# A graph kernel of eight rounds: another place for VectorE's list load, and one-hots that compare with a kept table

## The reference

```python
def _sage_conv(x, src, dst, Wl, bl, Wr, n_nodes):
    msg = x[src]
    summed = segment_sum(msg, dst, num_segments=n_nodes)
    cnt = segment_sum(ones((src.shape[0],)), dst, num_segments=n_nodes)
    mean = summed / maximum(cnt, 1.0)[:, None]
    return mean @ Wl + bl + x @ Wr
...
x = _layernorm(x + _L0_gnn_ref(...))   # three SAGE layers
x = _layernorm(x + _L1_gnn_ref(...))   # GIN: gelu(x[src] + edge_emb) * edge_weight, summed at dst, two-layer MLP
x = _layernorm(x + _L2_gnn_ref(...))   # two GCN layers, normalised by degree, layer norm with gain and shift
x = _layernorm(x + _L3_gnn_ref(...))   # two relational layers: one weight matrix for each of 8 edge types
```

## Time and profile before

| | |
|---|---|
| three runs | 5371.6, 5383.45 and 5387.2 us, median 5383.45 |
| the profiled execution | 5378.48 us, of which the span is 5376.4 |
| granted TensorE clock in it, mean | 0.944 of full speed |
| rounds 0 to 7, from their first one-hots | 471, 395, 579, 896, 610, 776, 750 and 852 us |

### The profile page before, as it was taken

The page is one execution under the profiler, slowest core; times in us unless marked ns, Lnnn a source line. Parts: engine busy times, 40 slices in busy tenths (PEclk is TensorE's granted clock), DMA queues, the critical chain, the costliest instruction groups (busy, mean ns, idle before and its releaser), DMA issues.

```text
span 5376.4 us, 129953 instructions
## 1 busy us (share of the span) xinstructions
PE 4387.9 (82%) x25128; PEld 2875.8 (53%) x25129; DVE 3446.8 (64%) x10510; ACT 2416.5 (45%) x4969; POOL 1921.9 (36%) x1886
## 2 busy tenths in 40 slices
PE   6998997777878888867777688887799996888895
PEld 4664554433445555535554355543577773677672
DVE  5553454787545555449997688876566663777774
ACT  2442442555257777526664466664222211333332
POOL 5650782654033333016550443310433312333310
PEclk9999999899889999989999899998899999999997
DMA  4663884665234444325553466653444433443432
GB/s 142 217 210 117 260 270 149 195 192 174 90 122 147 149 146 145 111 96 171 174 172 103 145 210 205 211 173 109 137 136 137 140 116 109 129 130 125 128 100 76
DMA packets 443919, 815.61 MB, mean 152 GB/s; under 512 B 70872, under 2 KB 76818, under 8 KB 443828
## 3 DMA queue, kind: packets, MB, share of 16 engines
q1 hardware_dynamic: 389172, 697.28, 38.4%
q0 software_dynamic: 54656, 117.32, 8.9%
HBM read 480.10 MB, written 334.22 MB: 151 GB/s over the span
## 4 chain that ended last, share of the span: by engine, by line
PE 46%; issue 15%; DVE 14%; DVEq 8%; ACT 7%; POOL 5%; DMA 3%; ACTq 2%; SPq 1%; POOLq 0%
PE p_agg L1132 8%; PE p_edge L1119 7%; PE p_agg L1134 7%; PE p_tr L1119 6%; POOL raw L696 4%; PE p_agg L1165 4%; DVE onehot L1566 4%; DVE stats L1658 3%; ACT u L916 2%; PE p_wide L1252 2%; ACT o L897 2%; DVEq L373 2%; PE p_agg L1158 2%; DVEq L1566 2%; PE p_dense L1208 2%
## 5 line engine op out<-in xcount | busy, mean ns | idle before, releaser
L1566 DVE TENSOR_SCALAR onehot<-iota,dst_f,negbase 128x512 f16<-128x512 f16 (+1 forms) x2848 | 1126.1, 449 | 815.6 <-PE p_agg L1165 305.3
L1132 PE MATMUL p_agg<-onehot,msg 128*128 128x512 f16 (+1 forms) x2848 | 1138.3, 400 | 596.5 <-DVE onehot L1566 338.6
L696 POOL DMA_INDIRECT raw<-node_s,src_i x980 | 958.7, 978 | 1449.1 <-DMA node_s<-o 561.4
L1134 PE MATMUL p_agg<-onehot,msg 128*128 128x512 f16 (+1 forms) x2848 | 1140.3, 400 | 0.0
L1132 PEld LDWEIGHTS p_agg<-onehot,msg 128*128 x2848 | 281.8, 99 | 941.4 <-issue 791.1
L696 POOL DMA_INDIRECT raw<-node_x,src_i x392 | 378.8, 966 | 551.0 <-DMA feature<-more_masked 253.6
L897 ACT ACTIVATE o<-v_ring,nmr,rstd 128x128 f32 (+1 forms) x1176 | 472.5, 482 | 76.6 <-DVE nmr L1674 71.5
L1165 PE MATMUL p_agg<-h_in,w 128*128 128x512 f32 x784 | 443.3, 649 | 22.9 <-DMA h_in<-feature 21.9
L1658 DVE BATCH_NORM_STATS2 stats<-v_ring 128x6 f32 (+1 forms) x1960 | 417.7, 278 | 44.3 <-DVE v_ring L1647 15.9
L916 ACT ACTIVATE u<-v_ring,nmr,rstd 128x128 f32 (+1 forms) x784 | 312.5, 481 | 225.0 <-DVE res_in L1704 134.7
L1134 PEld LDWEIGHTS p_agg<-onehot,msg 128*128 x2848 | 282.7, 99 | 219.1 <-issue 32.0
(11 more groups left out here) (260 smaller groups left out, 7741.9 us busy)
## 6 DMA issues: line engine op xcount, KB each, us to landing
node_s<-o SPq DMA_DIRECT2D x392, 256.0 KB
h_in<-feature SPq DMA_DIRECT2D x392, 256.0 KB
feature<-u SPq DMA_DIRECT2D x294, 256.0 KB
node_x<-o SPq DMA_DIRECT2D x294, 256.0 KB
res_in<-node_x SPq DMA_DIRECT2D x294, 256.0 KB
h_in<-node_s SPq DMA_DIRECT2D x196, 256.0 KB
h_t<-dinv_scratch SPq DMA_DIRECT2D x196, 256.0 KB
h_in<-in_x SPq DMA_DIRECT2D x98, 256.0 KB
```

What stands on the lines that cost most here:

```text
L696: nc.gpsimd.indirect_dma_start(out=raw[:, (e % RING) * BATCH + j, :], out_offset=None, in_=src_d, in_offset=bass.IndirectOffsetOnAxis(ap=s ...
L1132: nc.tensor.matmul(p_agg[:, a, :], tile_ap(msg, t, 0, D), oh, start=first, stop=True, skip_group_check=True)
L1134: return nc.tensor.matmul(p_agg[:, a, :], tile_ap(msg, t, D, 2 * D), oh, start=False, stop=True, skip_group_check=True)
L1566: return V.tensor_scalar(tile_ap(onehot, slot), iota[:, :], dst_f[:, bass.ds(t, 1)], negbase[:, bass.ds(it * 2 + a, 1)], ALU.subtract, ALU ...
```

## The change

A table `place` (128 x 294, f32) is added. Round 0 still uses the two-scalar compare; behind each half's three compares it writes the three sums `dst_f + negbase` to the table, with one 128x3 pass (98 of them). From round 1 on, `fixed` makes the three fixed one-hots of a half by comparing `iota` with a column of `place`, one scalar, whose address follows from the loop counter alone. Only the further groups (`further`) and the batches (`take_in`) still need the list; `list_of` loads it once a step, now for the following pair and in mid-step, and the step functions of rounds 1 to 7 are written anew around it with another starting point. The passes between engines and their semaphores stay; PE, ACT, POOL and SP have the same programs.

```diff
+        place = sb("place", [P, NHALF * EVERY])
...
+                def fixed(it, a):
+                    if not exists(it):
+                        return
+                    wait(dve, q.out_done, it * 2 + (a - 1))
+                    for j in range(EVERY):
+                        last = V.tensor_scalar(tile_ap(onehot, EVERY * a + j), iota[:, :],
+                                               place[:, bass.ds((it * 2 + a) * EVERY + j, 1)], None, ALU.is_equal)
+                    last.then_inc(q.every_ready.semaphore, 1)
...
                 def first_onehots(it, a, t0):
-                    if k:
-                        wait(dve, q.out_done, it * 2 + (a - 1))
-                    elif rel:
-                        wait(dve, q.turned, it * 2 + (a - 1))
                     for j in range(EVERY):
                         last = compare(it, a, EVERY * a + j, (t0 + j).with_bounds(min_val=0, max_val=TILES - 1))
                     last.then_inc(q.every_ready.semaphore, 1)
+                    V.tensor_scalar(place[:, bass.ds((it * 2 + a) * EVERY, EVERY)],
+                                    dst_f[:, bass.ds(t0.with_bounds(min_val=0, max_val=TILES - EVERY), EVERY)],
+                                    negbase[:, bass.ds(it * 2 + a, 1)], None, ALU.add)
...
+                def list_of(it):
+                    if exists(it + 1):
+                        return odd_list(dve, PT, it * 2 + 1)
+                    if exists(it):
+                        return None, (single_list(dve, PT, it * 2 + 1),)
+                    return None, ()
+                def take_in(these):
+                    if these[0]:
+                        each_batch(dve, *these[0], batch)
+                def further(it, a, these):
+                    if exists(it):
+                        more_onehots(it, a, these[1][1 - a][:3])
...
                 def second_gcn_step(it):
-                    now, after, ahead = next_items(it)
-                    if now:
-                        onehots(it + 1, now)
-                    scaled_sums(it, 1)
-                    statistics(it - 1, 0)
-                    statistics(it - 1, 1)
-                    scale_and_move(it - 1)
-                    if now:
-                        first_onehots(it + 1, 1, after)
-                    total_and_statistics(it - 2)
-                    scaled_sums(it + 1, 0)
-                    second_scale_and_move(it - 2)
                     gain_pass(it - 1)
-                    batches_ahead(ahead)
+                    these = list_of(it + 1)
+                    take_in(these)
+                    further(it + 1, 1, these)
+                    fixed(it + 2, 0)
+                    further(it + 2, 0, these)
+                    scaled_sums(it + 1, 1)
+                    statistics(it, 0)
+                    statistics(it, 1)
+                    scale_and_move(it)
+                    fixed(it + 2, 1)
+                    total_and_statistics(it - 1)
+                    scaled_sums(it + 2, 0)
+                    second_scale_and_move(it - 1)
...
+                def mean_step(it):
+                    statistics(it - 1, 0)
+                    add(it - 1, 1)
+                    these = list_of(it + 1)
+                    statistics(it - 1, 1)
+                    degrees(it, 1)
+                    fixed(it + 1, 1)
+                    scale_and_move(it - 1)
+                    add(it, 0)
+                    take_in(these)
+                    further(it + 1, 1, these)
+                    degrees(it + 1, 0)
+                    fixed(it + 2, 0)
+                    further(it + 2, 0, these)
```

More of the change, by code:

```diff
@@ L1594, in next_items @@
                         return None, None, None
[L1595 to L1601, removed]
+                    if exists(it + 2):
                         (e0, e1, e2), (now, after) = later_list(dve, PT, it * 2 + 1)
@@ L1612, in onehots @@
                 def onehots(it, these):
-                    if not rel:
-                        first_onehots(it, 0, these[0])
+                    first_onehots(it, 0, these[0])
                     more_onehots(it, 0, these)
@@ L1779, in gin_step @@
                 def gin_step(it):
+                    add(it, 0)
+                    these = list_of(it + 1)
+                    statistics(it, 0)
+                    take_in(these)
+                    further(it + 1, 1, these)
+                    fixed(it + 2, 0)
+                    further(it + 2, 0, these)
+                    add(it, 1)
+                    statistics(it, 1)
+                    scale_rows(it - 1)
+                    fixed(it + 2, 1)
+                    scale_and_move(it)
@@ new lines, in second_mean_step, with first_relational_step @@
+                def second_mean_step(it):
+                    fixed(it + 1, 1)
+                    these = list_of(it + 1)
+                    take_in(these)
+                    further(it + 1, 1, these)
+                    fixed(it + 2, 0)
+                    further(it + 2, 0, these)
+                def first_relational_step(it):
+                    fixed(it + 1, 1)
+                    these = list_of(it + 1)
+                    fixed(it + 2, 0)
+                    take_in(these)
+                    further(it + 1, 1, these)
+                    further(it + 2, 0, these)
@@ new lines, in second_relational_step, with first_list_taken @@
+                def second_relational_step(it):
+                    add(it, 1)
+                    these = list_of(it + 1)
+                    statistics(it, 1)
+                    fixed(it + 2, 0)
+                    take_in(these)
+                    further(it + 1, 1, these)
+                    further(it + 2, 0, these)
+                    scale_and_move(it)
+                    add(it + 1, 0)
+                    statistics(it + 1, 0)
+                    fixed(it + 2, 1)
+                def first_list_taken(these):
+                    if rel:
+                        fixed(1, 0)
+                    take_in(these)
+                    further(0, 1, these)
+                    degrees(0, 0)
+                    if not rel:
+                        fixed(1, 0)
+                    further(1, 0, these)
+                    if k >= 4:
+                        scaled_sums(0, 1)
+                        fixed(1, 1)
+                        if k == 5:
+                            scaled_sums(1, 0)
+                    elif k == 3:
+                        fixed(1, 1)
+                    elif rel and k == 2:
+                        add(0, 0)
+                        statistics(0, 0)
+                        fixed(1, 1)
@@ L1807, in step @@
[L1807 to L1840, removed]
+                    batches_ahead(ahead)
+                if not r:
+                    now, after = pair_list(dve, PT, 0)[0]
+                    first_onehots(0, 0, now[0])
+                    first_onehots(0, 1, after[0])
+                    early_batches(dve, PT, batch)
+                    more_onehots(0, 0, now)
+                    run_steps(dve, step)
+                    return
@@ L1841, in sage_round @@
+                wait(dve, S[r - 1].out_done, NHALF)
+                fixed(0, 0)
+                fixed(0, 1)
                 if k == 3:
```

37 lines of the change are left out of this document (17 added, 20 removed).

## The result

The changed kernel takes 5319.59 us (median of 4 runs, 5309.55 to 5331.12), the kernel before 5379.42 in the same series; the ratio is 0.9893, with a 95% interval of 0.9872 to 0.9914. It is faster, by about 60 us. The forecast was 118 us, so the direction was right and half the size is missing. The range of 5180 to 5345 holds the time because it reached past rival B, whose 5312 lies nearer to it than the forecast; whether B's reason is the right one is a question for the experiments.

The account below looks back on a forecast made before the run. DVE's sequence of passes was taken to set the step in rounds 2, 4 and 5, with PE following. Round 2 -48, round 4 -21, round 5 -23, rounds 3, 7, 6, 1 -29, round 0 +3: -118 from 5378.5 gives 5260.5 us; range 5180 to 5345.

Parts of the forecast that it names:

- rival B: Fixed compares: a second scalar costs nothing, so 51 us of the gain go, leaving -67: 5312 us; chance 0.18.
- (1): List load moved to mid-step, less the bare turn: -32 us in round 2, -5 in round 4, -7 in round 5.
- The price of the turn: DVE's loop turn, bare in rounds 2, 4 and 5: 0.4 us each, between 0.11 and 1.20 possible.
- C: Rival: the turn costs all of 1.20 us, 118 us given back in three rounds, 5378 us; chance 0.08.
- E: Rival: the load does not run beside the wide pass in three rounds, so slower, 5488 us; chance 0.09.
- Term (2): Fixed compare reads one scalar instead of two: 53 ns each, 15.6 us in each of rounds 2, 4 and 5.
- Term (3): Round 0 gets 98 additions to `place`, 15 us of passes, mostly under cover: +3 us, between 0 and +15.
- Term (4): The other rounds: -14 us in round 3, -10 in round 7, -3 in round 6, -2 in round 1.
- D: Rival: PE gains more, clock stays up and six tenths of its waits in rounds 2, 4, 5 go; 5172 us; chance 0.13.
- The sign of a third in both rounds: Sign that the forecast is right: PE's one-hot waits down by a third in rounds 2 and 4.

Follow-up runs that it names:

- E1: The changed kernel, but each fixed compare reads a second per-partition scalar again; 5369.68 us, ratio 0.9992 to the kernel before.
- E4: The changed kernel with the mid-step list load done twice in a row, in rounds from 1 on; 5423.31 us, ratio 1.0088.
- E3: The changed kernel with the loop's turn moved in rounds 2, 4 and 5, passes in the same cyclic order; 5272.47 us, ratio 0.9815.
- E2: The kernel before, order and list load kept, but fixed compares from round 1 on read the table with one scalar; 5336.08 us, ratio 0.9922.
- E7: As E6, but round 7's output stores follow both `h_in` loads and are those of one pair earlier; 5215.42 us, ratio 0.9704.
- E8: The kernel before, with only round 7's output stores put behind the loads of `h_in`; 5351.44 us, ratio 0.9956.
- E6: E3 plus, in round 7, both `h_in` loads for the next pair issued ahead of both `res_in` loads; 5279.51 us, ratio 0.9817.

## Why the prediction was wrong, step by step

**The term that failed is (1), the load.** It stood in the sum with -32 in round 2, -5 in round 4 and -7 in round 5. E1 measures the move without the cheaper compare: -19.6, +13.7 and +0.8, so that 39 of the missing 58 us lie here. Three things were left out or mis-sized.

- *The cover of the `add`.* The forecast set 0.69 us of pass against 0.75 of load and counted nothing bare. It took the load's length from the median of all rounds. At its new place in round 2 the load takes 1.30 us at the median, and starts 0.14 us after the `add`, so that 26.7 us stand behind the `add`. The turn's share of the 41.0 us is 14.3, less than the 20 forecast. E4 agrees that a load is not free there: a second one adds about 30 us to each of the three rounds.
- *The batch test.* Before, it ran behind the gain pass or `agg_t` without a load ahead of it. Behind the load it is late in every step with a batch: 6.2 us in round 4, and in round 5 the batch pass waits 16.5 us in 27 steps, 0.6 us each. The forecast had this in round 5, as up to 0.4 us, and not in round 4.
- *What follows a late pass.* In round 4 `shift` comes 0.44 us later, ACT's `v_ring` behind it, and DVE's statistics wait 12.7 us for that in place of 6.8. The forecast priced the bare turn and not who waits for the late pass.

**The price of the turn was right.** 0.4 us was taken, 0.44 was measured, 44 times in round 4. C and E, with a turn of 1.20 us or loads that run bare altogether, fell. E3 confirms the term from the other side: covered, it gives back 17.4 and 23.7 us.

**Term (2) was right in rounds 2, 4 and 5.** 53 ns were taken, 59 measured. The sum had 15.6 us in each of the three rounds; E2 gives 18.7, 18.7 and 19.6. So B fell, although its time was the nearest: that was chance, since of the 51 us that B took away E2 has 40, and most of what is missing is the load's. The rule of the Trainium skill in "VectorE: DVE Perf Modes", section "The TRN2 errata", has no term for a scalar, and this compare does not agree with it: 395 against 454 ns decide. The pair of 128x128 rows in f32 came near, though 59 lies above the 53 that the prediction gave as the upper end, and in part by luck: other rows of one form in that trace (98x98 in f32 with one column, two executions each) run from 262 to 308 ns.

**Term (3) was right.** The 98 additions raised DVE's busy time in round 0 from 269 to 289 us, and the round did not grow; they lie beside the waits of the earlier trace rows.

**Term (4).** Round 3 was right in sum (-11.9 for -14), and E1 and E2 show that it is the load's and not the compare's: -9.7 and -0.8, where the sum had -9.5 and -4.5. Rounds 1 and 6 stayed. In round 7 the prediction named the `h_in` wait, and counted it as a bound for the steady steps alone. It did more: in every one of E1 to E4 round 7 came out 7 to 19 us longer than before, and in the changed kernel's profiled execution, the fastest of four, 2 us shorter. PE's wait for `h_in` grew from 21.9 us to 39.4. Two such waits, before and after:

```profile
4763.53 1.12 PE L1165 MATMUL p_agg<-h_in,w 128*128 128x512 f32 x2 [1.96 <-DMA h_in<-feature]
```

```profile
4801.01 1.12 PE L1166 MATMUL p_agg<-h_in,w 128*128 128x512 f32 x2 [3.00 <-DMA h_in<-feature]
```

These loads were issued at 4759.43 and 4796.08: PE is ready for them about 2 us after the issue in both kernels, but the load lands 4.1 us after it before and 4.9 after. Over all such waits the median is 3.7 us before and 4.9 after. So the load became slower, and PE did not come sooner behind its issue. The `res_in` load ahead of it is issued 0.9 us closer to it than before; whether that is the reason was not tried. With the stores moved, E7 and E8 show the round's real share, 23 us.

**D** did not come: the granted clock of rounds 2, 4 and 5 is 0.87, 0.89 and 0.93, within 0.01 of the earlier trace rows, and of PE's waits for one-hots a fifth went in round 2 and a fourteenth in round 4, not six tenths. The sign of a third in both rounds failed with it.

Four things stay open. Round 7's length varied by 9 us between two executions with the same program for it (850.0 in the changed kernel, 859.2 in E3), and the change's size there is known to that only; round 4's varied by 7. Why the list load of round 2 takes longer at its new place, and why `h_in` lands later in round 7, was not tried. Nor was why round 5 gained 6 us less than its two parts.

## What to carry to other kernels

A load that the sequencer does is covered by what is left of the pass ahead at the moment it starts, less the tests behind it, and its length is to be taken from the place where it will stand: here it went from 0.75 to 1.30 us in one round. A loop's turn that a moved load leaves bare can cost as much as the move saves: 19.5 us came and 20.6 went in round 4. Cut the loop where a wide pass is in flight, and then look for who waits for the pass that became late. When one wait is shortened, take the transfer that ends next into the sum: here moving two stores behind a load gave as much as the whole change when the change was in (E6 to E7, 64 us), and 26 us without it (E8).

## What the runs showed of the hardware

- A second per-partition scalar in a 128x512 f16 compare on VectorE costs 59 ns: 454 against 395 in the mean, 407 against 348 at the median, and 58 to 60 at the median in each of rounds 1 to 7.
- The list load on DVE's sequencer took 0.75 us at the median over all rounds, before and after, but not at every place: in round 2 it went from 0.75 to 1.30 with the move, in round 1 from 1.14 to 0.76. In round 2 of the changed kernel it starts 0.14 us after the `add` ahead of it in most steps (an `add` at 1246.74 us, the load at 1246.88, done at 1247.63), so that the `add` covers 0.55 us of it, and up to 1.1 us stood idle behind the `add`.
- A loop's turn with no wide pass in flight delayed the next pass by 0.44 us (19.5 us in 44 steps).
- A 256 KB load issued 1.4 us behind two 256 KB stores in the same queue landed 5.5 us after its issue, and PE stood 3.6 us; in the kernel before, with the same stores ahead, such loads took 3.7 us at the median. With the stores issued behind the loads, no wait for `h_in` was left in the round.
